# The V projection of an attention and expert layer for two heads at once, in fp32r, and the order of the heads and batches around it

## What is computed

```python
q = rope(rmsnorm(x @ wq.T)); k = rope(rmsnorm(x @ wk.T)); v = x @ wv.T   # 16 heads of 128
scores = 50 * tanh(q @ k.T * 128**-0.5 / 50), masked above the diagonal
x = layernorm(x + softmax(scores) @ v @ wo.T)
x = layernorm(x + experts(x))
```

## Time and profile before

| | |
|---|---|
| median of three runs | 1137.06 us |
| the profiled execution | 1139.3 us, span 1137.5 us |
| mean granted clock of TensorE | 0.95 |
| TensorE matmuls busy | 1009.9 us, 89% of the span |
| VectorE | 843.9 us, 74% |
| ScalarE | 701.5 us, 62% |
| GpSimd | 634.0 us, 56% |
| DMA, mean / first slice | 58 GB/s / 328 GB/s |
| VectorE's subtractions prob_lo, 256 of them | 313.6 us, 1253 ns mean |
| GpSimd's additions into pacc (the 192 of the largest group) | 241.7 us, 1259 ns mean |
| V projection on TensorE, 1024 records | 124.6 us |

### The profile page before, as it was taken

How to read it: one execution, slowest core, us unless ns; L and a number is a source line. 1 busy time by engine, 2 the same in 40 slices (tenths; PEclk the granted TensorE clock), 3 DMA queues, 4 the chain that set the end, 5 groups by cost and what they waited for, 6 DMA issues and landing times.

```text
span 1137.5 us, 20522 instructions
## 1 busy us (share of the span) xinstructions
PE 1009.9 (89%) x6256; PEld 821.5 (72%) x6256; DVE 843.9 (74%) x1388; ACT 701.5 (62%) x1159; POOL 634.0 (56%) x668
## 2 busy tenths in 40 slices
PE   4688999999999999999999999999999869769700
PEld 3567888888888888888888888888888655345400
DVE  3377888888888889898989888888888856322206
ACT  3465777777777777777777777777777604212203
POOL 0255666666666666666666666666666742352322
PEclk9899999999999999999999999999999968979955
DMA  9000000011101010000000000001000059159235
GB/s 328 29 29 29 29 28 28 28 34 40 37 19 36 23 32 28 28 28 28 28 28 28 28 28 28 28 28 45 29 28 19 1 155 254 19 157 251 32 55 189
DMA packets 47322, 65.97 MB, mean 58 GB/s; under 512 B 8032, under 2 KB 38720, under 8 KB 47296
## 3 DMA queue, kind: packets, MB, share of 16 engines
q1 hardware_dynamic: 41200, 58.55, 16.7%
q0 software_dynamic: 3072, 4.46, 2.3%
q10 hardware_dynamic: 3024, 2.64, 0.7%
HBM read 54.35 MB, written 11.29 MB: 58 GB/s over the span
## 4 chain that ended last, share of the span: by engine, by line
PE 75%; DMA 11%; DVE 6%; issue 3%; POOL 2%; ACT 1%; SPq 1%; POOLq 0%; ACTq 0%; DVEq 0%
PE ps L372 20%; PE ps L373 19%; PE ps L374 19%; PE ps L400 9%; DMA acc_rows<-ye,acci 7%; PE ps L406 4%; PE ps L544 2%; DMA qsq<-rq_rows 1%; DMA yacc<-in_x 1%; DVE prob_lo L1002 1%; POOL pacc L894 1%; PE ps L554 1%; DVE qhat_lo L1002 1%; POOL xg L980 1%; POOL lnr L990 1%
## 5 line engine op out<-in xcount | busy, mean ns | idle before, releaser
L1002 DVE TENSOR_TENSOR prob_lo<-praw,prob_hi 128x1024 fp32r<-128x1024 f32 (+7 forms) x256 | 313.6, 1253 | 3.1 <-ACT prob_hi L681 3.1
L877 POOL TENSOR_SCALAR_AFFINE_SELECT praw<-praw 128x128 f32<-128x128 f32 x256 | 120.2, 471 | 306.5 <-ACT praw L728 288.9
L894 POOL TENSOR_TENSOR pacc<-pacc,praw 128x768 f32<-128x768 f32 (+2 forms) x192 | 241.7, 1259 | 16.6
L722 ACT ACTIVATE praw<-ps,rk 128x1024 f32<-128x1024 f32 (+7 forms) x256 | 185.9, 740 | 86.9 <-PE ps L374 82.8
L681 ACT ACTIVATE prob_hi<-praw 128x1024 fp32r<-128x1024 f32 (+7 forms) x256 | 168.0, 683 | 1.3 <-POOL praw L877 1.3
L728 ACT ACTIVATE praw<-praw 128x1024 f32<-128x1024 f32 (+7 forms) x256 | 167.5, 681 | 0.0
L372 PE MATMUL ps<-qhat_hi,kT_hi 128*128 128x512 f32 (+3 forms) x384 | 136.0, 354 | 13.7 <-DVE qhat_lo L1002 13.3
L372 PE MATMUL ps<-prob_hi,vS_hi 128*128 128x512 f32 (+3 forms) x384 | 136.3, 355 | 4.0 <-DVE prob_lo L1002 4.0
L373 PE MATMUL ps<-qhat_lo,kT_hi 128*128 128x512 f32 (+3 forms) x384 | 133.7, 348 | 0.0
L374 PE MATMUL ps<-qhat_hi,kT_lo 128*128 128x512 f32 (+3 forms) x384 | 133.7, 348 | 0.0
L373 PE MATMUL ps<-prob_lo,vS_hi 128*128 128x512 f32 (+3 forms) x384 | 133.5, 348 | 0.0
(11 more groups left out here) (151 smaller groups left out, 1938.1 us busy)
## 6 DMA issues: line engine op xcount, KB each, us to landing
qsq<-rq_rows SPq DMA_DIRECT2D x32, 512.0 KB, 3.8
wgu<-in_wgu SPq DMA_DIRECT2D x16, 704.0 KB
wd<-in_wd SPq DMA_DIRECT2D x16, 352.0 KB
wraw<-in_wqkv SPq DMA_DIRECT2D x16, 256.0 KB, 3.6
acc_rows<-pacc SPq DMA_DIRECT2D x8, 512.0 KB, 10.9
wv<-in_wqkv SPq DMA_DIRECT2D x16, 128.0 KB, 2.1
woraw<-in_wo SPq DMA_DIRECT2D x16, 128.0 KB, 2.1
yacc<-in_x SPq DMA_DIRECT2D x1, 2048.0 KB, 13.8
```

Source lines behind the costliest of these rows:

```text
L722: nc.scalar.activation(praw[:, raw_at(b, j)], buf[:, P * j:T], ACT.Tanh, scale=rk[:, b, j:j + 1]).then_inc(tanh_done, 1)
L877: nc.gpsimd.affine_select(out=diag, in_=diag, compare_op=ALU.is_ge, fill=0.0, base=0, pattern=[[1, P]], channel_multiplier=-1).then_inc(ma ...
L894: nc.gpsimd.tensor_tensor(pacc[:, P * j:T], before, raw, ALU.add).then_inc(pacc_done, 1)
L1002: v.tensor_tensor(dst, x_, hi.bitcast(F32), ALU.subtract).then_inc(done, 1)
```

## The change

- V is projected for two heads at once, from the split x and newly split V weights (`wv` becomes a pair of 256 columns), in three fp32r passes of 256 columns. A unit holds two tiles of 128 tokens for two heads; there are four for a pair of heads and a batch: vd (tiles 0 and 1), va (2 and 3), vb (4 and 5), vc (6 and 7). `vS` is laid out by tile and head.
- The steps are ordered by pairs of heads: head 0, head 1 of batch 0, then head 0, head 1 of batch 1 (q = 0 to 3; k = q % 2 is the head, b = q // 2 the batch).
- The loop's body has four steps; the first four and the last four are written out.
- va and vb are made in even steps, at the places of v0 and v1. vc is made in odd steps behind scores 0, and vd, for the next group, in odd steps between values 1 and scores 6. The prologue has one V unit in place of two.
- VectorE splits the V weights once in a pair, in step 3, behind tile 1. It splits the output weights at the start of steps 0 and 1, the query and key weights in steps 2 and 3, one head each.
- SyncE loads the weights of two heads by turns: V, then query and key, then output weights. `xraw` now lies in the space of `praw`, `gcur` has two columns, `wv_free` is gone.

```diff
-UNIT_ORDER = "q0 q1 k0 k1 ss sums op0 op1 v0 op2 op3 v1".split()
+STEPS = 4
+NP_ = H // 2
+EVEN = "q0 q1 k0 k1 ss sums op0 op1 va op2 op3 vb".split()
+ODD = "q0 q1 vc k0 k1 ss sums op0 op1 op2 op3 vd".split()
...
-                    for j in range(4):
-                        t0 = b * T + 512 * half + P * j
+                    for i in range(2):
+                        t0 = b * T + P * (2 * V_TILES[what] + i)
                         for c in range(KC):
-                            last = mm(bank[:, P * j:P * j + P], xraw[:, c, t0:t0 + P], wv[:, c, :], start=c == 0, stop=c == KC - 1)
+                            last = mm3(bank[:, 2 * DH * i:2 * DH * i + 2 * DH], of(xT, ALL, c, slice(t0, t0 + P)), of(wv, ALL, c, ALL),
+                                       c == 0, c == KC - 1)
...
# TensorE, step
+                scores(s, k, 0)
+                if k:
+                    project("vc", k, st.b, *st.unit("vc"))
...
+                scores(s, k, 5)
+                if not k:
+                    project("va", k, st.b, *st.unit("va"))
+                if old:
+                    out_proj(s - 1, 1 - k, 2, *st.unit("op2"))
+                values(s, k, 0)
+                if old:
+                    out_proj(s - 1, 1 - k, 3, *st.unit("op3"))
+                if not k:
+                    project("vb", k, st.b, *st.unit("vb"))
+                values(s, k, 1)
+                if k and new:
+                    if st.q == 3:
+                        pe.wait_ge(wvlo_done, st.pair + 2)
+                    project("vd", k, 1 - st.b, *st.unit("vd"))
+                scores(s, k, 6)
+                scores(s, k, 7)
+                values(s, k, 2)
...
# VectorE
+            def split_values_weights(p, count):
+
+                dve.wait_ge(wv_in, p * 32 + 32)
+                if count is not None:
+                    dve.wait_ge(pj_done, count)
+                src = wvraw[:, :, :, :].rearrange("p e c d -> p c e d")
+                by_head = [t[:, :, :].rearrange("p c (e d) -> p c e d", e=2) for t in wv]
+                v.tensor_copy(by_head[0], src).then_inc(wvhi_done, 1)
+                dve.wait_ge(wvhi_done, p + 1)
+                lo_of(by_head[1], src, by_head[0], wvlo_done)
...
+                if st.q < 2:
+                    split_output_weights(st)
                 if new:
-                    projected("q0", 1 - b, s + 1, *hd.unit(b, "q0"))
-                    projected("q1", 1 - b, s + 1, *hd.unit(b, "q1"))
-                if old:
-                    tile(s - 1, 1 - b, 4)
-                    tile(s - 1, 1 - b, 5)
-                    tile(s - 1, 1 - b, 6)
-                if old:
-                    tile(s - 1, 1 - b, 7)
+                    projected("q0", 1 - k, s + 1, *st.unit("q0"))
+                    projected("q1", 1 - k, s + 1, *st.unit("q1"))
+                if old:
+                    tile(s - 1, 1 - k, 4)
+                    tile(s - 1, 1 - k, 5)
+                if k:
+                    values_in("vc", st.group("vc"), *st.unit("vc"))
+                if old:
+                    tile(s - 1, 1 - k, 6)
+                    tile(s - 1, 1 - k, 7)
...
+                    if st.b and not st.last:
+                        split_next_weights(st.pair + 1, k, st.unit("q0")[0] - 1)
...
+                tile(s, k, 1)
+                if not k:
+                    values_in("va", st.group("va"), *st.unit("va"))
+                elif st.q == 3 and new:
+                    split_values_weights(st.pair + 1, st.unit("vc")[0])
...
+                    scale_raw(s + 1, 1 - k)
+                tile(s, k, 3)
+                if not k:
+                    values_in("vb", st.group("vb"), *st.unit("vb"))
+                elif new:
+                    values_in("vd", st.group("vd"), *st.unit("vd"))
                 if new:
+                    split_queries(s + 1, 1 - k)
...
+            with sp.Fori(0, NP_ - 1) as p:
+                sp.wait_ge(wvlo_done, p + 1)
+                for e in range(2):
+                    sp.dma_start(wvraw[:, e], ...).then_inc(wv_in, 16)
+                rq_broadcast(p * STEPS + 1, 1)
+                sp.wait_ge(wlo_done, p * 2 + 2)
+                for e in range(2):
+                    sp.dma_start(wraw[:, e], ...).then_inc(w_in[e], 16)
+                rq_broadcast(p * STEPS + 2, 0)
+                sp.wait_ge(wolo_done, p * 2 + 2)
+                for e in range(2):
+                    sp.dma_start(woraw[:, e], ...).then_inc(wo_in[e], 16)
+                rq_broadcast(p * STEPS + 3, 1)
+                rq_broadcast(p * STEPS + 4, 0)
```

## The result

The changed kernel takes 1206.97 us (median of 4 runs, 1202.93 to 1209.3) against 1135.44 for the kernel before on the same chip: a ratio on record of 1.0617, interval 1.0591 to 1.0642 (such ratios can differ from the quotient of the medians, here 1.063, by up to 0.3%). That is 71.5 us slower; I had forecast 39 and a range up to 1204. The profiled execution has a span of 1207.6 us.

A forecast was written before the change was run, and what follows sets the result against it. TensorE, busy for all 750 us of the middle stretch at full clock, was taken as the bound. -23.7 - 0.5 + 34.3 + 6.0 + 22.5 = +38.6 on 1137.06 gave 1176 us, range 1112 to 1204.

The forecast's parts named there:

- (b): Odd step's end: query split may meet GpSimd's accumulation; half of 15 lost at 3.0 us, +22.5 us, bounds 0 and 45.
- weight loads at cost 0: SyncE's loads: DMA sizes per head unchanged and waits early, so no queued broadcast is late; cost 0.
- (d): Output-weight split in step 1, behind an even step: a tie with GpSimd; 17 us if lost in 8 steps, taken as 0.
- (a): Start of a pair: output-weight split waits for GpSimd's accumulations, TensorE idles 3.2 us and loses clock; seven starts, +34.3 us.
- The clock: TensorE's slower clock behind stalls: 1.7 us lost per pair start, 0.8 us per lost query split, counted within those terms.
- vd's bank: Unit q1 of the next step waits for vd's eviction: 0.4 us in 15 steps, +6.0 us.
- V units: TensorE's 64 V projection units get cheaper, 1.42 us instead of 1.79 each: -23.7 us.
- Start, -0.5: Prologue: 512 KB more transfer ahead of yacc costs 1.6 us, one V unit fewer and a cheaper one save 2.2.
- (c): k1 waits for vc's eviction, done behind tile 5 amid the accumulations: 0 to 0.5 us in 16 steps, taken as 0.
- Rival 4: Four-step loop body not held on chip, fetched at 6 turns: +12 to +25 us on the forecast, 1188 to 1201; chance 0.04.
- Rival 3: Every contest between VectorE's splits and GpSimd lost, with (c) and (d): 1206 to 1223 us; chance 0.05.

The follow-up runs named there:

- e2: Changed kernel with GpSimd's seven long row-sum additions cut to 128 columns, output not the reference's: 1149.26 us, ratio 1.0068 to the kernel before.
- e12: Changed kernel with GpSimd's long additions cut to 128 columns and VectorE's loop over the middle pairs written out: 1123.33 us, ratio 0.9846.
- e14: As e12, with V evicted ahead of the remainder of tile 3 on VectorE: 1108.39 us, ratio 0.9755.
- e4: Changed kernel with only VectorE's loop over the middle pairs written out, real sums kept: 1198.88 us, ratio 1.0537.
- e15: Changed kernel with SyncE's three weight loads of a pair held until VectorE has split the queries of the step before: 1179.68 us, ratio 1.039.
- e5: Changed kernel with the output-weight split moved from the step's start to behind the transpose of the sums of squares: 1184.78 us, ratio 1.0376.
- e18: As e2, with VectorE's first middle pair written out ahead of its loop, so the same body stands elsewhere: 1116.94 us in a single run.
- e17: Changed kernel with the edits of e5 and e15, V evicted ahead of tile 3, VectorE's loop written out, TensorE's order kept: 1128.92 us, ratio 0.9902.
- e3: Kernel before with a loop body of four steps on TensorE, ScalarE, GpSimd and VectorE, nothing else: 1140.25 us, ratio 1.0002.

## Why the prediction was wrong, point by point

**Direction and mechanism were right**: slower, because the moved V units change who is first at GpSimd's additions. **The size was wrong**, +71.5 instead of +39. Two steps failed: the even chance given to the query race in (b), which was lost at all 15 ends, and the fetch of the longer body, 25 us, which stood outside the sum as a rival. A third, the weight loads at cost 0, bears on (b) and (d). (a), (d), the clock and vd's bank were off by less. Taking the exclusion away in steps gives a ledger of 24 steps: changed kernel 714.9, additions short (e2) 668.9, loop written out (e12) 643.2, V ahead of tile 3 (e14) 638.5; 24 x 2 x 0.36 = 17.3 us saved (1.79 us a unit before, 1.43 on average in e14, from start to start) would give 629.8. So the additions cost 46.0 us, the fetch 25.7, vd's bank 4.7, and 8.7 are left, whose cause stays open; 85.1 - 17.3 = 67.8. (The parts depend on the order in which they are taken away: the fetch alone, taken first, gave 18.4 in e4's profile; and each line carries the error of several us named above. By the ratios, additions and fetch are 5.5% and 2.2% of before over the whole kernel, 63 and 25 us.)

- *V units.* Right: a unit starts at 237.74 and the matmul behind it at 239.18 in the trace of after, 1.44 us against my 1.42.
- *Start, -0.5.* Step 4 at 158.48 against 158.73, but this is luck: the first step starts 1.1 us late (44.24 against 43.18), and the races of the first steps, which the term left out, fall differently on the way (e2, without them, has step 4 at 146.71).
- *(a) Output weights at a pair's start*, 7 x 3.2 us. The wait for q0's eviction is there each time, 1.7 to 3.8 us. At five of the seven it comes from the fetch as much as from the race (wo_lo 1.1 us behind 2.69 of issue).
- *(b) The query race*, half of 15 taken. It was lost at all 15. The price was near: of the twelve in the loop seven have cast and remainder long (2.6 and 2.7 us, TensorE waits 2.7) and five the remainder alone (3.0, TensorE waits 1.0 to 1.1), 2.0 us on average where I had 2.2. So was the rule: GpSimd's copy was issued 0.05 to 0.42 us ahead of the cast at every lost end, and 0.02 to 0.8 behind it at those that e15 wins. What failed is the tie: I had the cast at 530.29, by the one way of 6.15 us in the earlier trace rows, against the copy at 530.3. Over twelve ends of steps with b = 1 in the kernel before, steps 3 to 25, the way is 6.36 us on average (6.06 to 6.71), so the cast was due 0.2 us later, behind the copy, more often than not; "less than the broadcast varies" was no reason for a half. After the change it is 6.44 on average over such ends. At these ends a weight load stands close behind the broadcast in both kernels (0.87 us in the one before, at 524.03 and 524.90, 0.54 in the changed one).
- *The weight loads, cost 0.* I asked only whether SyncE's waits ahead of them were early. Early was the harm: with the loads behind the split 30.5 us of the loop come back (e15), 24.9 of them in the second steps of the pairs, where four of six query races and all six of (d) are won.
- *The clock.* I took 0.8 and 1.7 us for the two kinds of stall; at 276 to 286 us, with one of each, it was 3.3. Busy time times what the clock lacked, summed over rows of 1 us from 110 to 860, is 19 us after and 0 before.
- *vd's bank*, 15 x 0.4 = 6.0. The mechanism was right: 0.2 to 1.3 us, 6.7 us in 12 waits from 110 to 860, so 0.56 each, and 4.7 us of 24 steps by e14.
- *(c) vc's bank.* k1 waits 0.32 us for it in each second step of a pair, 2 us in all, within its bounds of 0 to 0.5.
- *(d) Output weights in step 1, a tie.* Lost every time in the loop: wo_lo takes 2.31 us, and vc waits 0.5 to 0.7 us for q0's eviction behind it, under the 2.1 that I had for a loss. The tie broke by the two loads of 256 KB, which the change put behind the broadcast of this step (way 6.52 us instead of 6.02, e15). (a) and (d) together are 2.4% of before, 27 us (e5), against 34.3 + 0.
- *Rival 4, the longer body.* It came true beside the forecast, not instead of it: 5 packets a turn on q14, on VectorE alone, 25 us, at the top of the 12 to 25 priced for it (for 6 turns back; there are 5). Its chance of 0.04 rested on a figure for how many instructions an engine holds. The figure of the Trainium skill (Runtime: NRT & Kernel Launch, "Instruction fetch mechanics"), 512 for VectorE, has room for the 273 of this body, and the body was fetched all the same at one place and not at another (e18). The same section of the Trainium skill says that instructions come in by blocks of 256 and that two such pages are held; by this a body of 273 can lie in two blocks or in three, according to where it begins. That would fit both kernels, but no run here shows where the blocks end. A size alone is no assurance. The earlier trace rows showed only that the two-step body at its place was held.
- *Rival 3, all races lost*, gave 1206 to 1223, and the time is in it, by luck: the fetch is in the time and not in this sum. With the fetch taken out it is 1198.88 (e4).

What stays open: which property of the place makes VectorE refetch; why the loop of e17 has only 1.6 us of the 17; and why an odd step with all its races won still takes 26.5 to 27.0 us in e14 where the passes sum to 26.2.

## What to carry to other kernels

When two engines exclude each other for a whole instruction, a schedule with 0.3 us between them is not safe under any reordering, even one that only saves work: take each margin from the mean and the spread of all its rows, and price a tie as lost at every end, since it can fall the same way each time (15 of 15 here). Look at what a DMA runs beside, not only at whether its wait is early. After changing a loop's body look at the instruction queues inside the loop, and if an engine shows issue time at the turn, move or unroll that loop before judging the change.

## What the runs showed of the hardware that I had not expected

- VectorE's loop of 273 instructions fetched 5 packets of 8 KB at each turn, three of them 2.4 us apart at the turn itself, and stood still for 2.5 to 2.9 us in the changed kernel and 4.0 to 4.4 in e2; the same body begun one pair later, and another of 274 instructions (e3), fetched none.
- Two weight loads of 128 KB issued 0.54 us behind a broadcast of 512 KB: the way of the factor is 6.45 us on average of six with them, 5.93 without. Two of 256 KB, 0.60 us behind: 6.52 with them, 5.94 without.
- After an idle time of 2.7 us, with 1.7 us more between, TensorE's granted clock was 0.50 for 8 us and 0.76 for the next 4 (rows at 276 to 288 us), although it was busy for 10 of these 12 us.
